# A transformer layer on one core: TensorE's 28 middle units written out without a loop

## The chip, the cores and the metric

The kernel runs on one core of one Trainium2 chip. The metric is the device time of the whole program in microseconds (us). Three timed runs of the kernel before gave 1525.46, 1525.85 and 1527.17 us; the median is 1525.85 us.

A core has five engines that run their own instruction streams and meet only at semaphores: TensorE (PE in the profile, its weight loads PEld), VectorE (DVE), ScalarE (ACT), GpSimd (POOL) and SyncE (SP). A "q" behind the name, as in PEldq or SPq, is the part of an engine that handles register operations, branches, waits and the issue of DMAs.

## The reference

The layer is one attention block and one feed-forward block over hidden states of 4 x 512 x 512 in float32:

```python
x = x + _layernorm(attn(_layernorm(x)))   # 32 query heads, 8 key/value heads, head size 128
x = x + _layernorm(ffn(_layernorm(x)))    # width 1376, silu(gate) * up, then down

# attn: the weights are integer codes with one scale per 128 input rows
w = (codes - 8.0) * repeat(scales, 128)
q, k, v = x @ w_q, x @ w_k, x @ w_v       # rope on q and k, each k/v head serves 4 query heads
p = softmax(q @ k.T * 128 ** -0.5 + causal_mask)
out = (p @ v) @ w_o
```

## The kernel before, in words

Every float32 operand of a matmul is split into a high and a low float16 half, and each product is made of three matmuls (hi x hi, lo x hi, hi x lo), or of two where the weight is exact. The attention runs as 32 units, `UNITS = NKV * NB`: unit U stands for one key/value head and one batch, four units of the same head in a row. A unit has four steps h, one for each query head; head number n is `4 * U + h`. All engines go through the same 32 units, each with a program of its own.

On TensorE (the function `unit` under `@block.tensor`, from line 904) a step issues, in this order:

- `attend` (lines 856 to 869) for head n-2: 30 matmuls of 128 columns, from the transposed probabilities in `ffn_w` into `ps_o`. It waits for `oq_norm` (line 858), `pt_hi_in` and `pt_lo_in` (the two DMA transposes of the probabilities), and `piece_dve`.
- `scores` (lines 841 to 853) for head n+1, into `ps_s`, in three parts, and between these parts
- `out_tile` (lines 934 to 954) for head n-3: the matmuls of the output projection, lines 837 and 838. The first of them waits for `ot_in` at line 942, the DMA transpose of the attention output (`ot<-o_parts` in the rows), and each for its bank of `ps_p`.
- one or two pieces of the next unit's projections (K, V or one of Q0 to Q3; lines 813 to 815 and 829 to 831), and the fourth output tile.

`ps_p` is a ring of four banks that VectorE empties. The two buffers of `wo` and of the projection weights change every four units, so that TensorE's loop body holds NB = 4 units.

The loop is `pe.Fori(0, UNITS // NB - 1)` at line 990: seven passes of four units, with units 0 and 1 ahead of it and units 30 and 31 behind it, these four written out. In the loop the unit number is a value of a register: `NB * p + 2 + i`. So the semaphore count that a wait needs is worked out in a register, and so is the half of the weights, in `half = (V >> 2) & 1` (`project`, `project_v`) and in `output`. The helper `after` (line 153) leaves out a wait that asks for zero when its value is a plain number, and always waits when it is a register's value:

```python
def after(eng, sem, value):
    if isinstance(value, int) and value <= 0:
        return
    eng.wait_ge(sem, value)
```

VectorE has a loop of the same four units a pass (line 1290), ScalarE, GpSimd and SyncE have loops of two units (lines 747, 586 and 457). SyncE issues nearly all DMAs, in the order of its program: in step n the swaps for rope (lines 375, 376), the transposes of the probabilities of head n (lines 385, 391), the transpose of the attention output of head n-2 (line 400), and once a unit the next weights (lines 353, 356, 365). The chain behind one head goes TensorE `scores`, VectorE `lows` (L1152), ScalarE `exps` and `p_high` (L650, L659), GpSimd `p_low` (L511), SyncE's transposes, TensorE `attend`, ScalarE `o_norm` (L667), GpSimd `o_parts` (L519), SyncE's transpose (L400), TensorE `out_tile`.

Of the kernel before, what the change touches and what calls it, by code (L numbers as in the profile page):

```python
# [29 lines left out]
NB, S, D = 4, 512, 512  # L30
# [6 lines left out]
UNITS = NKV * NB  # L37
# [33 lines left out]
FULL = (("K", "Q0"), ("Q1",), ("Q2", "V"), ("Q3",))  # L71
# [92 lines left out]
def layer(nc, x, w_codes, w_scales, o_codes, o_scales,  # L164
          gate_t, gate_s, up_t, up_s, down_t, down_s, cos_t, sin_t, ident_in, mask_in, out):
    ctx = ExitStack()
    with ctx:
# [620 lines left out]
        def _(pe):  # L788
# [198 lines left out]

            unit(0, 0, FULL, first=True)
            unit(1, 1, FULL)
            with pe.Fori(0, UNITS // NB - 1) as p:  # L990
                for i in range(NB):
                    unit(NB * p + 2 + i, (2 + i) % NB, FULL)
            unit(UNITS - 2, NB - 2, FULL)
            unit(UNITS - 1, NB - 1, LAST, last=True)

            outs = outs_before(UNITS) + 3 * KT
# [416 lines left out]
```

## Time and profile before

| | |
|---|---|
| Median of 3 timed runs | 1525.85 us |
| Profiled execution, span from first to last instruction | 1530.4 us |
| TensorE busy | 1427.8 us, 93% of the span, 11104 matmuls |
| VectorE, ScalarE, GpSimd busy | 72%, 65%, 65% |
| Mean granted TensorE clock | 0.983 of full speed |
| Queue q8, kind "instruction" | 109 packets, 1.79 MB |

The profile gives no time of its own for the profiled execution beside the span. The span is 4.55 us longer than the median of the timed runs.

The attention fills the time to about 1290 us, the feed-forward block the rest. TensorE's loop runs from 138 us to 1188 us. The share of busy time says that TensorE is the engine with the least idle time; what the idle time in the loop is made of is told by the waits, the timeline and the windows, whose rows stand below. In such rows a matmul's duration runs to a modelled end: two matmuls of 512 columns in a row start 0.22 us apart although each is shown as 0.38 us long.

### The profile page before, as it was taken

To read this page: it belongs to the slowest core of one execution; us is meant where nothing else is said; L and a number is where in the kernel's file an instruction comes from. 1 tells how busy PE (TensorE), PEld (TensorE's weight loads), DVE (VectorE), ACT (ScalarE), POOL (GpSimd) and SP (SyncE) were. 2 spreads that over 40 slices of the span, in tenths; PEclk is the share of its full clock that TensorE was granted. 3 is DMA by queue.
4 is the path that set the end of the run, shared out by engine and by line. 5 is a ranking of instruction groups with operands and counts; after the bars stand their busy time and mean duration, and the time that the engine had idled before them with its cause. 6 is when DMAs were issued, how large, how long until landed. Compare 5 with 4: busy or idle time off the path is not lost.

```text
span 1530.4 us, 40795 instructions
## 1 busy us (share of the span) xinstructions
PE 1427.8 (93%) x11104; PEld 851.8 (56%) x11104; DVE 1096.3 (72%) x2469; ACT 994.9 (65%) x2582; POOL 1000.8 (65%) x704
## 2 busy tenths in 40 slices
PE   5778899999999999999999999999999967999998
PEld 2444466556556665666566656665666643454543
DVE  7746577777777777777777777777777786776744
ACT  2566577777777777777777777777777862332321
POOL 2467678878887787888788878887888851110100
PEclk9999999999999999999999999999999998999999
DMA  8379989989888888888899888988989864011000
GB/s 268 67 150 163 168 168 173 165 162 169 168 160 165 167 172 160 168 169 167 157 166 169 164 160 162 165 161 158 169 165 172 167 123 91 14 48 42 15 28 28
DMA packets 522609, 217.10 MB, mean 142 GB/s; under 512 B 478944, under 2 KB 480704, under 8 KB 522432
## 3 DMA queue, kind: packets, MB, share of 16 engines
q1 hardware_dynamic: 519968, 210.53, 71.3%
q0 software_dynamic: 2464, 4.23, 1.9%
q8 instruction: 109, 1.79, 0.5%
q14 instruction: 68, 0.56, 0.1%
HBM read 55.32 MB, written 4.19 MB: 39 GB/s over the span
## 4 chain that ended last, share of the span: by engine, by line
PE 71%; DMA 8%; SPq 7%; issue 6%; POOL 3%; DVE 2%; ACT 2%; DVEq 0%; POOLq 0%; ACTq 0%
PE ps_p L813 7%; PE ps_p L815 7%; PE ps_p L814 7%; PE ps_p L837 6%; DMA ot<-o_parts 6%; PE ps_p L838 6%; PE ps_s L1049 4%; PE ps_s L1048 4%; PE ps_s L850 3%; PE ps_s L851 3%; PE ps_s L852 3%; PE ps_o L866 3%; PE ps_o L868 3%; PE ps_o L867 3%; PE ps_p L1062 2%
## 5 line engine op out<-in xcount | busy, mean ns | idle before, releaser
L511 POOL TENSOR_TENSOR p_lo<-prob,p_hi 128x1280 f16<-128x1280 f32 x128 | 335.8, 2623 | 179.2 <-ACT p_hi L659 146.5
L1139 DVE SCALAR_TENSOR_TENSOR y<-ps_p,wo_scale,y 128x512 f32<-128x512 f32 x512 | 380.5, 744 | 81.5 <-PE ps_p L838 79.2
L650 ACT ACTIVATE prob<-prob,exp_bias 128x512 f32<-128x512 f32 (+3 forms) x512 | 285.5, 558 | 12.5
L1152 DVE CUSTOM_DVE_ANT_0 prob<-ps_s,mask 128x512 f32<-128x512 f32 (+3 forms) x512 | 237.0, 482 | 70.5 <-PE ps_s L852 69.4
L813 PE MATMUL ps_p<-x_hi,w_hi 128*128 128x512 f16 x640 | 245.2, 383 | 3.6 <-DVE w_lo L1073 1.5
L837 PE MATMUL ps_p<-ot,wo 128*128 128x512 f16 x512 | 198.8, 388 | 49.9 <-DMA ot<-o_parts 41.7
L814 PE MATMUL ps_p<-x_lo,w_hi 128*128 128x512 f16 x640 | 244.9, 383 | 0.0
L815 PE MATMUL ps_p<-x_hi,w_lo 128*128 128x512 f16 x640 | 244.8, 382 | 0.0
L866 PE MATMUL ps_o<-v_hi,ffn_w 128*128 128x128 f16 x1280 | 221.2, 219 | 9.1 <-DVE rot L1127 8.1
L867 PE MATMUL ps_o<-v_lo,ffn_w 128*128 128x128 f16 x1280 | 221.0, 219 | 0.0
L868 PE MATMUL ps_o<-v_hi,ffn_w 128*128 128x128 f16 x1280 | 221.0, 219 | 0.0
L667 ACT ACTIVATE o_f<-ps_o,inv_sum 128x128 f32<-128x128 f32 x512 | 146.1, 368 | 114.8 <-PE ps_o L868 111.7
L1124 DVE TENSOR_TENSOR other<-ps_p,sin 128x512 f32<-128x512 f32 x160 | 109.5, 685 | 151.7 <-PE ps_p L815 150.4
L495 POOL TENSOR_TENSOR rot<-rot,swap 128x512 f32<-128x512 f32 x160 | 203.3, 1279 | 17.8 <-DMA swap<-other 17.6
L838 PE MATMUL ps_p<-ot,wo 128*128 128x512 f16 x512 | 198.9, 388 | 0.0
L552 POOL TENSOR_TENSOR rstd<-ve,minus_half 128x1 f32<-128x1 f32 x48 | 26.4, 551 | 250.1 <-DVE ve L1209 250.1
L659 ACT ACTIVATE p_hi<-prob 128x1280 f16<-128x1280 f32 x128 | 162.7, 1271 | 23.9 <-DMA ffn_w<-p_hi 19.0
L519 POOL TENSOR_TENSOR o_parts<-o_f,o_parts 128x512 f16<-128x512 f32 x128 | 149.0, 1164 | 38.9 <-ACT o_parts L671 38.9
L503 POOL TENSOR_TENSOR q_lo<-rot,q_hi 128x512 f16<-128x512 f32 x128 | 170.3, 1331 | 2.6 <-ACT q_hi L632 2.6
L850 PE MATMUL ps_s<-k_hi,q_hi 128*128 128x512 f16 (+3 forms) x512 | 155.6, 304 | 9.3 <-POOL q_lo L503 6.8
L851 PE MATMUL ps_s<-k_lo,q_hi 128*128 128x512 f16 (+3 forms) x512 | 155.5, 304 | 0.0
L852 PE MATMUL ps_s<-k_hi,q_lo 128*128 128x512 f16 (+3 forms) x512 | 149.1, 304 | 0.0
(102 smaller groups left out, 2942.5 us busy)
## 6 DMA issues: line engine op xcount, KB each, us to landing
swap<-other SPq DMA_DIRECT2D x320, 128.0 KB, 2.7
w_code<-w_codes SPq DMA_DIRECT2D x36, 384.0 KB, 3.3
w_scale<-w_scales SPq DMA_DIRECT2D x36, 384.0 KB, 4.6
o_code<-o_codes SPq DMA_DIRECT2D x35, 256.0 KB, 2.9
swap<-x SPq DMA_DIRECT2D x16, 256.0 KB, 2.8
out<-z SPq DMA_DIRECT2D x16, 256.0 KB, 2.0
ffn_w<-x SPq DMA_DIRECT2D x3, 1024.0 KB, 9.5
ffn_w<-p_hi SPq DMA_TRANSPOSE x128, 3.5
```

The costliest lines, as they stand in the source:

```text
L511: pool.tensor_tensor(p_lo[:, :], prob[:, hp, :], p_hi[:, :], ALU.subtract).then_inc(p_lod, 1)
L650: act.activation(prob[:, hp, a:a + w], prob[:, hp, a:a + w], ACT.Exp, bias=exp_bias[:, hp, i:i + 1], scale=-1.0, accum_out=exp_sum[:, hp, ...
L813: pe.matmul(ps_p[:, bank, :], wh, xh, start=(k == 0), stop=False)
L814: pe.matmul(ps_p[:, bank, :], wh, xl, start=False, stop=False)
L815: mm = pe.matmul(ps_p[:, bank, :], wl, xh, start=False, stop=(k == KT - 1))
L837: pe.matmul(ps_p[:, bank, :], w, flat(ot[:, hp, 0:TT, :]), start=True, stop=False)
L838: pe.matmul(ps_p[:, bank, :], w, flat(ot[:, hp, TT:2 * TT, :]), start=False, stop=True).then_inc(o_ps, 1)
L866: pe.matmul(o, ph, vh, start=(i == ORDER[0] and j == 0), stop=False)
L867: pe.matmul(o, ph, vl, start=False, stop=False)
L868: mm = pe.matmul(o, pl, vh, start=False, stop=(i == ORDER[-1]))
L1139: dve.scalar_tensor_tensor(tile, ps_p[:, bank, :], scale, tile, ALU.mult, ALU.add).then_inc(o_add, 1)
L1152: dve.tensor_tensor_reduce(prob[:, hp, P_AT[i]:P_AT[i] + w], ps_s[:, bank, col:col + w], mask[:, S - w:], -SCORE_SCALE, NO_MINIMUM, ALU.ad ...
```

## The change

The loop around TensorE's 28 middle units is replaced by a Python `for`, so that these units are written out in the program with plain numbers in place of the register's value. Nothing else is edited; the loops of the other engines stay.

```diff
@@ -987,10 +987,8 @@
 
             unit(0, 0, FULL, first=True)
             unit(1, 1, FULL)
-            with pe.Fori(0, UNITS // NB - 1) as p:
-                for i in range(NB):
-                    unit(NB * p + 2 + i, (2 + i) % NB, FULL)
-            unit(UNITS - 2, NB - 2, FULL)
+            for U in range(2, UNITS - 1):
+                unit(U, U % NB, FULL)
             unit(UNITS - 1, NB - 1, LAST, last=True)
```

The first place is on TensorE, where unit 1 ends and the loop's first unit begins. `L837` and `L838` are the last output tile of unit 1, `L866` to `L868` the first matmuls of `attend`, `ISA` a register operation or wait that the queue handles. Before:

```order
L838 MATMUL ps_p<-ot,wo 128x512
L990 UNCONDITIONAL_BRANCH
L990 ISA
L858 ISA [waits oq_norm]
L860 ISA [waits pt_lo_in,pt_hi_in]
L866 MATMUL ps_o<-v_hi,ffn_w 128x128 [waits piece_dve]
L867 MATMUL ps_o<-v_lo,ffn_w 128x128
```

In the changed kernel:

```order
L837 MATMUL ps_p<-ot,wo 128x512 [waits o_add]
L838 MATMUL ps_p<-ot,wo 128x512
L866 MATMUL ps_o<-v_hi,ffn_w 128x128 [waits pt_lo_in,piece_dve,pt_hi_in,oq_norm]
L867 MATMUL ps_o<-v_lo,ffn_w 128x128
L868 MATMUL ps_o<-v_hi,ffn_w 128x128
```

The branches are gone, and the register operations of `attend` with them; the four waits stand ahead of the first matmul. The matmuls are the same.

The second place is on TensorE in the first unit of the loop body, between the scores and the first output tile, which waits for the transposed attention output. Before:

```order
L843 ISA
L157 ISA [waits rot_lo]
L850 MATMUL ps_s<-k_hi,q_hi 128x512 [waits low_done]
L851 MATMUL ps_s<-k_lo,q_hi 128x512
L852 MATMUL ps_s<-k_hi,q_lo 128x512
L157 ISA
L942 REGISTER_ALU [waits o_add]
L837 REGISTER_ALU [waits ot_in]
L837 REGISTER_ALU
L837 ISA
L837 MATMUL ps_p<-ot,wo 128x512
```

In the changed kernel:

```order
L850 MATMUL ps_s<-k_hi,q_hi 128x512 [waits low_done,rot_lo]
L851 MATMUL ps_s<-k_lo,q_hi 128x512
L852 MATMUL ps_s<-k_hi,q_lo 128x512
L837 MATMUL ps_p<-ot,wo 128x512 [waits ot_in,o_add]
L838 MATMUL ps_p<-ot,wo 128x512
```

The waits for `ot_in` and `o_add` stood on register operations, with two more of these between the wait for `ot_in` and the matmul; now both stand right ahead of the matmul.

## Rows read from the trace of the kernel before

**Rows 1.** The page's busy time by engine, and its slices of the span.

```profile
PE 1427.8 (93%) x11104; PEld 851.8 (56%) x11104; DVE 1096.3 (72%) x2469; ACT 994.9 (65%) x2582; POOL 1000.8 (65%) x704
...
PE   5778899999999999999999999999999967999998
...
PEclk9999999999999999999999999999999998999999
```

**Rows 2.** TensorE's waits, 303 to 1188 us: us in total, times, longest.

```profile
PE ps_p L837 <- DMA ot<-o_parts: 9.9, 16, 1.4
PE ps_o L866 <- DVE rot L1127: 8.1, 5, 1.7
PE ps_p L837 <- issue: 1.5, 4, 0.7
PE ps_o L866 <- DMA ffn_w<-p_lo: 1.0, 1, 1.0
PE ps_p L813 <- issue: 0.4, 2, 0.2
```

**Rows 3.** Queue instructions of line 990: count, duration ns min/median/max, first and last start.

```profile
L990 PEldq COMPARE_BRANCH  x7: 83/4457/4605, 298.7 to 1184.6; - x7
```

**Rows 4.** TensorE's timeline around two loop ends: start us, duration, idle before and releaser.

```profile
301.86 0.38 PE L838 MATMUL ps_p<-ot,wo 128*128 128x512 f16 x1
303.23 0.23 PE L866 MATMUL ps_o<-v_hi,ffn_w 128*128 128x128 f16 x1 [0.99 <-DMA ffn_w<-p_lo]
...
450.75 0.38 PE L837 MATMUL ps_p<-ot,wo 128*128 128x512 f16 x1
450.97 0.38 PE L838 MATMUL ps_p<-ot,wo 128*128 128x512 f16 x1
453.04 0.23 PE L866 MATMUL ps_o<-v_hi,ffn_w 128*128 128x128 f16 x1 [1.70 <-DVE rot L1127]
```

**Rows 5.** The timeline where the loop is left, 1187.4 us on.

```profile
1187.67 0.38 PE L838 MATMUL ps_p<-ot,wo 128*128 128x512 f16 x1
1187.88 0.22 PE L866 MATMUL ps_o<-v_hi,ffn_w 128*128 128x128 f16 x1
```

**Rows 6.** Stretches: length, PE, PEld, DVE, ACT, POOL busy; clock, DMA share, GB/s.

```profile
453.04:599.94 146.90, 143.90 (x1233) 89.79 (x1233) 109.68 (x257) 113.44 (x304) 120.08 (x81) 1.00 0.89 166
599.94:747.29 147.35, 144.06 (x1233) 89.79 (x1233) 109.94 (x257) 113.13 (x304) 120.47 (x81) 1.00 0.89 166
747.29:894.46 147.17, 144.02 (x1233) 89.77 (x1233) 109.61 (x257) 113.33 (x304) 120.22 (x81) 1.00 0.90 166
1042.54:1187.88 145.34, 143.85 (x1232) 89.89 (x1233) 108.03 (x255) 111.81 (x303) 119.84 (x80) 1.00 0.89 166
1187.88:1223.64 35.76, 35.76 (x310) 22.58 (x308) 27.34 (x65) 28.34 (x79) 30.07 (x20) 1.00 0.90 168
```

**Rows 7.** The chain of waits around 541 us and around 1241 us: start, us, what.

```profile
541.23 5.08 DMA ot<-o_parts
546.32 0.24 issue
546.55 0.39 PE ps_p L837
...
1241.72 3.11 DMA ot<-o_parts
1244.83 0.14 issue
1244.97 0.58 PE ps_p L837
```

**Rows 8.** The chain of waits around 484 us.

```profile
483.47 0.22 PE ps_s L852
483.68 0.37 issue
484.06 0.39 PE ps_p L837
```

**Rows 9.** SyncE's timeline around the loop end at 450 us, and the tile that needs it.

```profile
448.77 1.33 SPq L400 DMA_TRANSPOSE ot<-o_parts  x1
...
455.37 0.38 PE L837 MATMUL ps_p<-ot,wo 128*128 128x512 f16 x1
```

**Rows 10.** Instruction fetches of one pass, 453.04 to 599.94 us, and of unit 30.

```profile
q8 instruction: 13, 0.21, 0.6%
...
q8 instruction: 3, 0.05, 0.5%
```

**Rows 11.** The branch of VectorE's loop, with as many passes as TensorE's.

```profile
L1290 DVEq COMPARE_BRANCH  x7: 60/68/68, 302.9 to 1188.7; - x7
```

**Rows 12.** SyncE's waits over the whole span, the three that belong to the loop.

```profile
SPq L390 <- POOL p_lo L511: 82.3, 38, 4.6
SPq L374 <- DVE other L1124: 80.8, 62, 10.1
SPq L399 <- POOL o_parts L519: 73.1, 48, 4.5
```

## The prediction

> **What bounds the kernel now.** I read the page's busy shares first, then TensorE's waits in the loop, then the timeline at the places that the change touches, and last the stretches of one pass each. The page shows TensorE busy 93% of the span with the granted clock near full speed in almost every slice [rows 1]. In the middle of the loop it is denser still: a pass of four units takes 146.90 to 147.35 us, of which 143.90 to 144.06 are busy [rows 6]. VectorE is busy 110 us of such a pass, ScalarE 113, GpSimd 120 and the DMA engines 89%. So TensorE sets the pace, and a pass has only about 3 us in it that are not matmuls.
>
> The waits say what these 3 us are [rows 2]. From 303 to 1188 us, six passes, TensorE idled 9.9 us in 16 waits for the transposed attention output, 8.1 us in five waits ahead of L866 that are put down to VectorE's L1127, 1.0 us in a sixth that is put down to a transpose, and 1.9 us in six waits called issue. The wait ahead of L866 is the one to look at, since L1127 writes `rot`, which `attend` doesn't read. The timeline places it: the last matmul of a pass starts at 450.97, the first of the next pass at 453.04 [rows 4]. The queue has a compare-and-branch of line 990 seven times, with a median of 4457 ns and a minimum of 83 ns [rows 3]. Six of the seven are taken. Where the loop is left, L866 follows L838 after 0.21 us, which is the plain distance of two matmuls, with no idle time at all [rows 5]. So the branch that falls through costs the array nothing, the taken ones hold TensorE's queue for more than 4 us, the array works off about 3 us of matmuls already queued, and the rest is a hole. The releaser named at each hole is only whatever ended last elsewhere.
>
> **The change, part by part.**
>
> Taken branches. One hole is 453.04 - 450.97 = 2.07 us from start to start, less the 0.22 us that the matmul would have taken anyway: 1.85 us. The first is 303.23 - 301.86 - 0.22 = 1.15 us [rows 4]. For the six, the idle times are 8.1 + 1.0 = 9.1 us [rows 2]. Those count from a modelled end that lies 0.38 - 0.22 = 0.16 us after the next possible start, so 6 x 0.16 = 1.0 us comes on top: 10.1 us. A second reading agrees: the last pass, which ends without a taken branch, takes 145.34 us, the three others 147.14 on average, a difference of 1.80 us at equal busy time [rows 6]. I take 10.1 us.
>
> Register operations at a wait. In the loop the first output tile starts 0.24 us after the transpose has landed, outside the loop 0.14 us [rows 7]. The code there is the same but for the register operations, so 0.10 us for each wait that binds: 16 in the waits of six passes [rows 2], 19 by scale for seven, 1.9 us. The waits called issue are the longer form, four register operations: 0.37 us with nothing to wait for [rows 8]. There are four at L837 (1.5 us) and two at L813 (0.4 us) [rows 2]. I count half of these 1.9 us, since a landing a little later may bind there instead. For waits too short for that list I count nothing. That makes 2.8 us, with bounds of 0 (everything is caught by the next landing) and 4.5 us (all of both and 0.7 us for the short ones).
>
> Fetching the program. 28 units in a row are some seven times the code of the loop body. This costs nothing if the loop streams its code already, and it does: one pass fetched 13 packets, 0.21 MB, and the written-out unit 30 fetched 3, the same rate, and was busy 35.76 of 35.76 us while it did [rows 6, 10]. With fewer register operations and no fetch repeated at a branch the total should fall from 109 packets to between 90 and 97. I take 0, with bounds of -1 and +4 us (a stall of 0.05 us at each of some 80 blocks).
>
> What is late next. A transfer that was begun before a loop end and is needed behind it doesn't move when the hole goes. The transposes of the probabilities are needed steps later. The close one is the attention output: issued at 448.77, needed at 455.37 [rows 9], and 1.85 us earlier without the hole, that is at 453.52. One such transpose took 5.08 us to land, another 3.11 [rows 7]; the landing is then at 451.9 to 453.85, so at worst some 0.5 us of the 1.85 turn into a wait. Further back everything is tied to TensorE: SyncE waits mostly for GpSimd's and VectorE's results [rows 12], whose inputs are TensorE's. The hole also lets GpSimd catch up, which is 82% busy in a pass. I put what is given back at 2 us for all six holes together, with bounds of 0 and 10.1 us.
>
> Sum: -10.1 - 2.8 + 0 + 2 = -10.9 us against the profiled span of 1530.4 us, so 1519.5 us. The span lies 4.55 us over the median of the runs, and I assume that offset to stay: 1525.85 - 10.9 = 1514.9 us.
>
> [...]
>
> **The rivals.**
>
> A, the DMA side takes it back. DMA engines are 89% busy in every pass [rows 6], and the waits for `ot` are the largest item in the list [rows 2]. If the pace of SyncE's queue were the true limit, each hole that closes would open as a longer wait for `ot`. For it speaks that 16 such waits exist; against it that unit 30 ran 35.76 us without one idle moment at a share of 0.90 [rows 6], and that those waits last 0.6 us on average (9.9 / 16), as chains that start at TensorE. Full give-back leaves only part of the register term: about 1524 to 1526 us; half of it leaves 1520.
>
> B, slower: the straight code is fetched too late. TensorE needs a new block of code about every 12 us (146.90 / 13 = 11.3) [rows 6, 10]. If the next block came late each time by a time s, some 80 blocks in the former loop would cost 80 s. It decides from 12.9 / 80 = 0.16 us a block; at 0.25 us a block the time is 1525.85 - 12.9 + 20 = 1533 us. For it speaks that the DMA engines that bring the code are 89% busy; against it the dense unit 30, and that the loop's inside shows idle time only at L837, L813 and L866 [rows 2], which are waits in the program and no block borders.
>
> C, a taken branch costs as little as the untaken one and the holes come from a semaphore that is late at each loop end. Then the holes stay, and the register term alone gives 1525.85 - 2.8 = 1523 us. For it speaks the releaser named, L1127; against it that L866 at 1187.88, the same place in the program, has no hole [rows 5]. [...]
>
> D, all waits shrink more than counted, since a reaction sooner on TensorE is a start sooner for the whole chain behind it: all of both terms and nothing given back, -10.1 - 4.5 = -14.6, 1511.3 us.
>
> **How the numbers follow.** The forecast as worked out, from 1512.5 to 1518.5 us, has a chance of 0.70; D and what lies under it 0.10; a half or full give-back (A) 0.12; C 0.04; B 0.04. The range has to hold 8 in 10: from 1511 us (inside D) to 1520.5 us (half of A). A measurement can tell 0.2% from no change, 3.05 us: 1522.8 to 1528.9 us count as the same. Faster are the forecast, D and about half of A's and C's chance: 0.88. The same are the rest of A and C and a weak B: 0.09. Slower: 0.03.
>
> **What would show it.** No compare-and-branch of line 990 in TensorE's queue. No idle time ahead of L866 at the former loop ends, and all passes of four units near 145 us, with TensorE busy 144. The first output tile 0.14 us after its landing in the former loop. The queue q8 with 90 to 97 packets. TensorE's waits for `ot` in the loop still 10 to 12 us: if they are 18 or more, A is right. If idle time appears at places without a wait, in a rhythm of some 12 us, B is. If L866 still has a hole at every sixteenth head, C is. The prediction is wrong if the time is above 1520.5 us, or if it is right by a term that is none of these.

## The result, and the profile after

The changed kernel takes 1516.51 us (median of 5 runs, 1515.25 to 1521.49) against 1525.85 us before: a ratio of 0.9938, 95% interval 0.9918 to 0.9957, or 9.3 us less. In a second group of runs (f0_after) it was 1515.40 us against 1526.38, ratio 0.9927 (0.9911 to 0.9943). The forecast was 1514.9 us, the range 1511 to 1520.5.

The page of the changed kernel answers to [rows 1], its queue q8 to the 109 packets of before:

```profile
PE 1423.1 (94%) x11104; PEld 853.0 (56%) x11104; DVE 1094.0 (72%) x2469; ACT 992.9 (66%) x2582; POOL 1000.6 (66%) x704
...
q8 instruction: 89, 1.46, 0.4%
```

TensorE's waits from the first matmul of unit 6 to that of unit 30, the same six passes as in [rows 2]; columns are us in total, times, longest:

```profile
PE ps_p L837 <- DMA ot<-o_parts: 11.7, 14, 1.6
PE ps_p L813 <- DVE w_lo L1071: 0.4, 2, 0.2
```

The 9.1 us ahead of L866 are gone, and so are the waits called issue. What was 16 waits of 9.9 us for the attention output is now 14 waits of 11.7 us: fewer and longer. Three passes of four units, and the last, answer to [rows 6] (length, then the busy time of PE, PEld, DVE, ACT, POOL, the granted clock, the DMA share):

```profile
443.04:588.25 145.21, 143.50 (x1233) 90.07 (x1232) 109.58 (x257) 112.70 (x305) 120.23 (x80) 1.00 0.87 168
588.25:733.46 145.21, 143.51 (x1234) 90.06 (x1232) 109.55 (x257) 112.95 (x305) 120.22 (x80) 1.00 0.88 168
733.46:881.03 147.57, 144.00 (x1234) 89.86 (x1232) 109.43 (x257) 113.58 (x305) 120.16 (x80) 1.00 0.91 166
...
1026.24:1170.96 144.72, 143.34 (x1233) 90.15 (x1232) 108.99 (x257) 112.93 (x305) 120.23 (x80) 1.00 0.86 167
```

The two profiled spans, 1530.4 and 1513.4 us, differ by 17.0 us, more than the medians. The run of the second profile is 1.85 us longer than its span (1515.25 against 1513.4), and the others are 1.7 to 1.9 us longer, so the profiled execution of before took about 1532.2 us. That is above all five runs of its own group (1525.38 to 1527.73) and about as long as the longest of before in the group of e1_hint (1532.07). To compare what repeats I split the time at the first matmul of units 1, 3 and 31. Of before and of the changed kernel:

```profile
99.60:192.77 93.17, 76.12 (x617) 46.20 (x616) 54.05 (x129) 59.81 (x165) 61.04 (x42) 0.93 0.93 163
192.77:1223.64 1030.87, 1008.14 (x8626) 628.55 (x8624) 767.62 (x1793) 793.34 (x2131) 841.87 (x560) 1.00 0.89 166
```

```profile
99.07:188.27 89.20, 73.62 (x618) 45.13 (x617) 53.68 (x129) 59.71 (x165) 61.02 (x42) 0.94 0.88 170
188.27:1206.72 1018.45, 1005.03 (x8625) 630.18 (x8624) 765.83 (x1793) 791.51 (x2131) 841.48 (x560) 1.00 0.88 167
```

Units 1 and 2, in which the first feed-forward weights are loaded, differ by 4.0 us; in the other profiles below they took from 87.4 to 91.9 us. The 28 units from 3 to 30, called "the stretch" from here on, went from 1030.87 to 1018.45 us, 12.4 us less, and the second profile of the changed kernel has 1018.55. The medians give 9.3 and 11.0 us, so some of the 12.4 may belong to the long execution of before. The six holes alone were 10.1 us in that profile. This looks like the forecast come true. The experiments show that it is not.

### The profile page after: what moved, and what is told of

Its sections match the earlier page's. It is cut to its first block, busy times and chain, and to the rows that moved or that the text cites. A ratio compares the mean times of both kernels' runs of the same rounds, so it can differ in the third digit from the quotient of the medians.

```text
span 1513.4 us, 38106 instructions
## 1 busy us (share of the span) xinstructions
PE 1423.1 (94%) x11104; PEld 853.0 (56%) x11104; DVE 1094.0 (72%) x2469; ACT 992.9 (66%) x2582; POOL 1000.6 (66%) x704
## 4 chain that ended last, share of the span: by engine, by line
PE 69%; DMA 7%; issue 7%; SPq 5%; POOL 5%; DVE 3%; ACT 2%; DVEq 1%; POOLq 0%; ACTq 0%
PE ps_p L813 7%; PE ps_p L815 7%; PE ps_p L814 7%; PE ps_p L837 6%; PE ps_p L838 5%; DMA ot<-o_parts 4%; PE ps_s L1046 4%; PE ps_s L1047 4%; PE ps_s L852 3%; PE ps_s L850 3%; PE ps_s L851 3%; PE ps_o L868 3%; PE ps_o L867 3%; PE ps_o L866 3%; PE ps_p L1060 2%
## 5 line engine op out<-in xcount | busy, mean ns | idle before, releaser
L813 PE MATMUL ps_p<-x_hi,w_hi 128*128 128x512 f16 x640 | 244.6, 382 | 2.8 <-DVE x_lo L1105 1.4
L837 PE MATMUL ps_p<-ot,wo 128*128 128x512 f16 x512 | 198.3, 387 | 48.6 <-DMA ot<-o_parts 42.0
L868 PE MATMUL ps_o<-v_hi,ffn_w 128*128 128x128 f16 x1280 | 221.0, 219 | 0.0
L866 PE MATMUL ps_o<-v_hi,ffn_w 128*128 128x128 f16 x1280 | 221.0, 219 | 0.0
L495 POOL TENSOR_TENSOR rot<-rot,swap 128x512 f32<-128x512 f32 x160 | 202.5, 1274 | 16.8 <-DMA swap<-other 16.8
L838 PE MATMUL ps_p<-ot,wo 128*128 128x512 f16 x512 | 198.6, 388 | 0.0
L850 PE MATMUL ps_s<-k_hi,q_hi 128*128 128x512 f16 (+3 forms) x512 | 155.3, 303 | 8.0 <-POOL q_lo L503 5.5
```

The source lines that it names most:

```text
L813: pe.matmul(ps_p[:, bank, :], wh, xh, start=(k == 0), stop=False)
L837: pe.matmul(ps_p[:, bank, :], w, flat(ot[:, hp, 0:TT, :]), start=True, stop=False)
L838: pe.matmul(ps_p[:, bank, :], w, flat(ot[:, hp, TT:2 * TT, :]), start=False, stop=True).then_inc(o_ps, 1)
L866: pe.matmul(o, ph, vh, start=(i == ORDER[0] and j == 0), stop=False)
L868: mm = pe.matmul(o, pl, vh, start=False, stop=(i == ORDER[-1]))
```

## The experiments

The stretch by kernel (one profile each), the matmul-to-matmul time lost in it at holes ahead of L866 and at all other waits over 0.2 us, and the ratio of the timed runs to those of before. Loss is the distance of two starts less the distance that such a pair has without a wait. A profile is of one execution, up to 5.2 us over the median of its runs (f4_bothhint, 1523.45 against 1518.26), so a stretch by itself tells no differences of a few us.

| kernel | stretch us | holes | other waits | ratio, 95% interval |
|---|---|---|---|---|
| before | 1030.87 | 10.06 | 18.87 | |
| the change | 1018.45 | 0 | 16.83 | 0.9938 (0.9918 to 0.9957) |
| the change, second group (f0_after) | 1018.55 | 0 | 17.06 | 0.9927 (0.9911 to 0.9943) |
| TensorE's loop with a hint (e1_hint) | 1028.66 | 0 | 26.52 | 0.9988 (0.9976 to 1.0000) |
| single passes, registers kept (e2_single) | 1024.27 | 0 | 22.74 | 0.9968 (0.9955 to 0.9982) |
| four passes, rest written out (e3_half) | 1023.34 | 4.90 | 16.53 | 0.9952 (0.9935 to 0.9968) |
| loop end behind attend (e4_edge) | 1060.48 | 28.5, ahead of L850 | | 1.0199 (1.0181 to 1.0218) |
| the change, near branches (e5_short) | 1023.14 | 0 | 21.10 | 0.9939 (0.9917 to 0.9962) |
| TensorE, VectorE written out (f1_both) | 1009.97 | 0 | 8.55 | 0.9855 (0.9833 to 0.9878) |
| the change, VectorE's loop with a hint (f3_dvehint) | 1009.30 | 0 | 7.90 | 0.9865 (0.9843 to 0.9887) |
| both loops with a hint (f4_bothhint) | 1022.11 | 0 | 20.05 | 0.9944 (0.9926 to 0.9962) |
| only VectorE written out (f2_dve) | 1029.68 | 6.55 | 21.07 | 0.9989 (0.9975 to 1.0004) |
| all five written out (f5_all) | 1009.98 | 0 | 8.4 | 0.9837 (0.9812 to 0.9861) |
| both written out, padded (f6_pad) | 1018.91 | 0 | 15.09 | 0.9926 (0.9905 to 0.9948) |

**e1_hint: the branch without the wait for its code.**

```diff
-            with pe.Fori(0, UNITS // NB - 1) as p:
+            with nc.Fori(0, UNITS // NB - 1, engines=[pe.engine], hint_back_edge=True) as p:
```

> The loop of before is kept, with a prefetch hint for the branch at its end. Measure: the stretch from the first matmul of unit 3 to that of unit 31, 1030.9 us in the profile of before and 1018.5 us in that of the changed kernel, and the median time. Theory (a taken branch waits for the code of the loop's top to be fetched, and the hole is that time less the matmuls already queued): the six branches fall from 4.4 us to under 1 us, the holes ahead of L866 to under 0.3 us, the register operations stay; stretch 1020 to 1022 us, time 1517 to 1520 us. Rival (a taken branch on TensorE is slow by itself, or a semaphore is late at the loop end): the holes stay at 1.2 to 1.9 us, stretch 1030 us, time 1525 to 1527 us.

The median was 1526.11 us, 1.8 us under the 1527.93 us of before in its group. The queue's instructions of line 990 (count, duration ns min/median/max) answer to [rows 3]:

```profile
L990 PEldq BRANCH_PREFETCH_HINT  x7: 36/36/45, 134.3 to 1030.6; - x7
L990 PEldq COMPARE_BRANCH  x7: 88/353/389, 294.6 to 1177.7; - x7
```

TensorE's waits from unit 3 to 31 (us in total, times, longest):

```profile
PE ps_p L837 <- DMA ot<-o_parts: 16.7, 23, 1.7
PE ps_p L837 <- issue: 2.3, 6, 0.7
```

The mechanism holds: a hinted branch takes 0.35 us instead of 4.46, and no hole is left ahead of L866. So I take the 4.46 us for a wait for code; in e5_short below a taken branch to a loop head a few instructions back lasted 0.21 to 0.24 us. But the time hardly fell, and did not reach the theory's 1517 to 1520 us; it is the rival's time, without the rival's holes: the other waits grew from 18.9 to 26.5 us. 10.1 us of holes were taken away and 7.7 came back.

**e2_single: no branch back, all register operations.**

```diff
-            with pe.Fori(0, UNITS // NB - 1) as p:
-                for i in range(NB):
-                    unit(NB * p + 2 + i, (2 + i) % NB, FULL)
+            for q in range(UNITS // NB - 1):
+                with pe.Fori(q, q + 2, 2) as p:
+                    for i in range(NB):
+                        unit(NB * p + 2 + i, (2 + i) % NB, FULL)
```

> Seven loops of a single pass in a row: every group of four units is written out, but the unit number is still a register's value, so all register operations stay and no branch back is taken. Theory (register operations cost 0.1 to 0.3 us at each wait that binds, 2 to 3 us in all): no hole ahead of L866, the first output tile still 0.24 us after its landing, stretch from unit 3 to unit 31 1020.5 to 1021.5 us, 2 to 3 us over the changed kernel; time 1517 to 1520 us. Rival (only the branches count, what the register operations delay is caught by the next landing): stretch 1018 to 1019 us, time as the changed kernel, 1516.5 us.

Median 1522.04 us, 4.9 us under before by the ratio. The stretch is 5.8 us longer than that of the changed kernel, not 2 to 3 (4.6 us by the ratios): registers cost about twice what I had counted. Set against e1_hint, which has the same register operations and a hinted branch, it is 4.4 us shorter (3 us by the ratios, whose intervals overlap). It had 99 fetches where e1_hint had 104; why the two differ stays open.

**e3_half: three taken branches instead of six.**

```diff
-            with pe.Fori(0, UNITS // NB - 1) as p:
+            with pe.Fori(0, 4) as p:
                 for i in range(NB):
                     unit(NB * p + 2 + i, (2 + i) % NB, FULL)
-            unit(UNITS - 2, NB - 2, FULL)
+            for U in range(18, UNITS - 1):
+                unit(U, U % NB, FULL)
```

> The loop does four passes (three taken branches), units 18 to 30 are written out. Theory: about half of the gain, three holes of 1.2 to 1.9 us (4.6 us in all) and the register operations of 16 units: stretch from unit 3 to unit 31 1024 to 1025 us, time 1520 to 1522 us. Rival (the DMA side takes back what is gained, so that the gain is no sum over holes): units 18 to 31 show waits for the attention output that are longer by as much as the holes that are gone, and the stretch from unit 18 on is no shorter than in before (476.3 us).

Median 1521.00 us, stretch 1023.34 us. From unit 18 to unit 31 it took 471.1 us (740.94 to 1212.05) against 476.3 before, so part of the gain is kept where the loop is gone. It keeps three fifths of the gain by the stretches (7.5 of 12.4 us) and three quarters by the ratios (7.3 of 9.5 us), both more than the theory's half; the intervals of the ratios reach 2.5 to 3 us to either side.

**e4_edge: the same loop, its end behind short matmuls.**

```diff
+            attend_ahead(2, 2)
             with pe.Fori(0, UNITS // NB - 1) as p:
                 for i in range(NB):
-                    unit(NB * p + 2 + i, (2 + i) % NB, FULL)
-            unit(UNITS - 2, NB - 2, FULL)
+                    unit(NB * p + 2 + i, (2 + i) % NB, FULL, attended=(i == 0))
+                attend_ahead(NB * p + 6, 2)
+            unit(UNITS - 2, NB - 2, FULL, attended=True)
```

`attend_ahead` issues the first `attend` of the unit, which `unit` then leaves out.

> The loop is kept but its end moved behind the 30 short matmuls (56 ns each) of the first attend of a unit. Theory (hole = branch time less the matmuls queued at it): some 14 matmuls are queued, now worth 0.8 us in place of 3 us, so each of six holes grows from 1.7 to about 3.7 us and stands behind the last L868 instead of ahead of the first L866; stretch from unit 3 to 31 about 1041 us, time 1536 to 1538 us, less what the waits for the attention output catch. Rival (a semaphore that attend waits for is late at each fourth unit): the hole stays ahead of L866 at 1.2 to 1.9 us, time 1525 to 1527 us.

Median 1557.69 us, 30 us over before, more than forecast. The branch at its new line:

```profile
L996 PEldq COMPARE_BRANCH  x7: 83/5111/5949, 298.0 to 1213.5; - x7
```

TensorE's waits, 300 to 1165 us:

```profile
PE ps_s L850 <- issue: 14.7, 3, 5.2
PE ps_s L850 <- POOL q_lo L503: 12.8, 3, 4.3
```

And the 12 us around one loop end, in the columns of the passes above:

```profile
600.50:612.50 12.00, 7.27 (x48) 3.96 (x47) 6.47 (x10) 5.44 (x16) 6.81 (x4) 0.76 1.06 183
```

The holes moved with the branch to where it now stands, and grew from 1.7 to 4.7 us on average: 27.5 us by these rows, which count from modelled ends, and 0.16 us more for each. The matmuls queued ahead of the branch are short, and the branch itself took 4.9 to 5.9 us instead of 4.0 to 4.6. So the hole goes with the branch and the work queued ahead of it, and no semaphore of the first `attend` makes it; three of the six are put down to `q_lo`, but all six have the branch in front. The rest of the loss is the clock: the granted clock was 0.76 in the 12 us around this hole and 0.72 to 0.86 in the same stretch of the five others. It was 0.50 for 3.4 us at three of the six holes and for 6.8 us at the other three (at this one from 606.7 to 613.5 us), and matmuls of 512 columns in a row started 0.43 us apart there instead of 0.22; in the kernel before it was 1.00 in each pass [rows 6]. So TensorE's busy time in the stretch rose from 1008.14 to 1019.12 us.

**The second theory.** The waits that came back in e1_hint are not spread evenly. In the changed kernel 11.1 of the 16.8 us lie in units 6, 10, 14, 18, 22 and 26, the units that begin a pass of the loops still kept. In e1_hint it is 11.7 of 26.5 and in e2_single 12.0 of 22.7; in the kernel before these six units had 5.2 us of such waits beside the 10.1 us of holes. So in these three kernels, where TensorE's holes are gone and VectorE's loop is as it was, 6 to 7 us come back in the very units behind the holes. The chain of waits of the changed kernel leads from there to VectorE (start, us, what):

```profile
443.89 0.07 DVEq L1288
443.95 0.28 issue
444.24 0.74 DVE y L1137
444.98 2.50 DVE w_lo L1071
447.47 0.39 issue
447.86 0.07 DVEq L1288
447.94 0.05 issue
...
449.62 0.55 DVE prob L1150
450.17 1.56 issue
451.73 0.06 DVE low L1150
...
453.91 0.67 DVE other L1122
...
459.11 1.68 SPq L391
...
461.07 3.74 DMA ot<-o_parts
464.81 0.14 issue
464.95 0.38 PE ps_p L837
```

L1288 is the head of VectorE's loop. Its branch at 443.89 is shown as 0.07 us, yet the first instruction behind it, of the same line, starts at 447.86, 3.97 us later. I read this as a wait for code like TensorE's, only that VectorE's record of the branch, 0.07 us, doesn't contain the wait. Two instructions already queued cover most of it, then VectorE stands still, and once more for 1.56 us at 450.17. The DMA packets show the fetches: on queue q14, whose packets of 8 KB become fewer when VectorE is written out (68 on the page, 42 in f1_both), one started 2.15 us after this branch and the next 6.0 us after it. In the kernel before the first of them started 2.3 to 2.6 us behind each of VectorE's six taken branches. The row that shows VectorE's stall in the kernel before, 300 to 1170 us, is

```profile
DVE low L1152 <- issue: 8.7, 6, 2.1
```

In the changed kernel the stall delays the scores' minimum, then the rope of the next pieces, then SyncE's queue, and ends at 464.95 as a wait of TensorE of 1.59 us. In the kernel before, both engines fetched at the same loop end, and by this theory TensorE's hole hid VectorE's.

**f1_both, f3_dvehint and f4_bothhint, with f0_after as their measure.** f0_after is the changed kernel again. f1_both adds

```diff
-            with dve.Fori(0, UNITS // NB - 1) as p:
-                for i in range(NB):
-                    unit(NB * p + 2 + i, (2 + i) % NB, FULL)
-            unit(UNITS - 2, NB - 2, FULL)
+            for U in range(2, UNITS - 1):
+                unit(U, U % NB, FULL)
```

f3_dvehint instead keeps VectorE's loop as `nc.Fori(..., engines=[dve.engine], hint_back_edge=True)`, and f4_bothhint is the kernel before with such a hint on both loops.

> The changed kernel again, as the measure for the other runs of this group. Time 8 to 11 us under before; stretch from the first matmul of unit 3 to that of unit 31 within 2 us of 1018.5 us.

> TensorE's and VectorE's middle units are both written out. New theory: VectorE's loop end is a fetch too (its branch is shown as 68 ns, but its queue starts the next operation 4.5 us later, and VectorE then idles 1 to 2 us in a wait called issue); TensorE's hole covered it, and in the changed kernel it comes back as a wait for the attention output of 1.8 to 2.2 us in units 6, 10, 14, 18, 22, 26. By it these waits fall under 1 us: stretch from unit 3 to 31 1007 to 1012 us, time 6 to 11 us under the changed kernel. Rival (the DMA side sets these waits): they stay, stretch 1016 to 1019 us, time within 2 us of the changed kernel.

> The changed kernel, VectorE's loop kept with a prefetch hint for its branch: only the fetch is taken away, VectorE's register operations stay. New theory: VectorE's queue goes on within 1 us of the branch, the waits of 1.8 to 2.2 us in units 6, 10, ..., 26 fall under 1.2 us, time 4 to 8 us under the changed kernel. Rival (DMA side, or VectorE's register operations rather than its fetch): time within 2 us of the changed kernel.

> Both loops kept, both with a prefetch hint; all register operations stay. With the hint on TensorE alone the time fell only 1.8 us. New theory: with VectorE's fetch gone too the six holes really go, time 7 to 11 us under before. Rival (the register operations on TensorE were the larger part of the change): time 1 to 3 us under before, as with the hint on TensorE alone.

Medians 1515.40, 1505.59, 1505.18 and 1518.26 us, against 1526.38 us before. TensorE's waits from unit 3 to 31 with the hint on VectorE (f3_dvehint):

```profile
PE ps_p L837 <- DMA ot<-o_parts: 4.8, 7, 1.1
PE ps_p L837 <- issue: 0.8, 1, 0.8
```

VectorE's waits called issue in it, 300 to 1165 us:

```profile
DVE prob L1150 <- issue: 0.3, 1, 0.3
```

And in the changed kernel, 300 to 1170 us:

```profile
DVE low L1150 <- issue: 7.9, 6, 2.2
...
DVE prob L1150 <- issue: 4.7, 5, 1.2
```

So 12.6 us of standing still on VectorE became 0.3, and TensorE's other waits fell from 17.1 to 7.9 us; in the six units behind the loop ends they fell from 11.4 us (f0_after) to 1.4, to 0.9 with VectorE written out and to 0.3 with both hints. VectorE's queue did not go on within 1 us of the branch, as expected, but after 2.0 to 3.4 us, its first code packet started 0.1 to 1.6 us behind the branch, and the gain of 10 us was above the 4 to 8 expected. The hint does as much as writing VectorE out (0.9865 and 0.9855, their intervals overlap), so it is the fetch and not VectorE's register operations. This edit is worth some 10 us on top of the change, as much as the change that this study is about. With both hints and all registers (f4_bothhint) the time is 8.1 us under before, where the hint on TensorE alone had brought 1.8: the holes are worth their price once the stall beneath them is gone too.

**f2_dve: the cover from the other side.** The kernel before with VectorE's edit of f1_both alone.

> The kernel before with VectorE's middle units written out and TensorE's loop kept. Theory (the two engines' fetches lie at the same loop end and cover each other): TensorE's six holes of 1.2 to 1.9 us stay and hide most of what VectorE's were worth, time 0 to 4 us under before, where the same edit was worth 9.8 us on top of the changed kernel. Rival (the two are independent sums): 8 to 11 us under before.

Median 1528.48 us against 1529.38, ratio 0.9989 (0.9975 to 1.0004). The same edit that is worth 10 us beside the change is worth nothing measurable without it. TensorE's holes shrank from 10.1 to 6.6 us, and its other waits rose by 2.2. Of two stalls that lie over each other, taking away either alone gains at most 1 to 2 us (the interval of this one holds zero, that of e1_hint touches it), and both together 8.1 us (f4_bothhint).

**f5_all: the other three engines.** ScalarE's, GpSimd's and SyncE's loops written out as well.

> All five engines' middle units written out. The branches of ScalarE, GpSimd and SyncE delay the next queue operation by only 0.26 to 0.33 us, fourteen times each, and their register operations 0.04 to 0.1 us each. Theory (these lie in the chain from the scores to the transpose that TensorE waits for): 1 to 4 us under the kernel with TensorE and VectorE written out. Rival (they have idle time beside the chain): within 1 us of it.

Median 1505.49 us, ratio 0.9837 (0.9812 to 0.9861); f1_both in its own group had 0.9855 (0.9833 to 0.9878). The intervals overlap, and the stretches are equal (1009.98 and 1009.97 us). No gain is shown. The ratios by themselves would leave room for one of 2 to 3 us; the equal stretches speak for the rival.

**f6_pad: a longer program without register operations.** To f1_both it adds, in `project` four times and in `project_v` six times for each k,

```diff
+                    if V > 2:
+                        for _ in range(4):
+                            pe.sem_inc(pe_passed)
```

> TensorE's and VectorE's middle units written out as in the earlier run, and TensorE's program made longer again by some 104 semaphore increments a unit that nobody waits for, placed among the projection matmuls where they hide, none at a wait. Theory (the register operations also cost by the length of the program: a 16 KB fetch of TensorE's code that meets the transpose of the attention output lands it 0.8 to 1.0 us later, and a longer program has more of them): 109 fetches where the changed kernel has 89, waits for the attention output up, time 2 to 6 us over the kernel with both written out. Rival (the register operations cost only what stands between a landing and the matmul): time within 1.5 us of it.

Median 1518.42 us, ratio 0.9926, so 11 us over f1_both by the ratios. It doesn't settle its question. It had 101 fetches, not 109, and the waits for the attention output became fewer, not more. The rows are TensorE's waits in it, 300 to 1160 us:

```profile
PE ps_p L814 <- DVE w_lo L1078: 0.9, 3, 0.4
PE ps_p L844 <- issue: 0.9, 5, 0.2
```

Instead every unit loses 0.28 us on average ahead of the same output tile, and 0.18 us more in the V piece, whose matmuls start 56 ns apart: the increments did not hide where I had put them. What it shows is that some 0.46 us a unit lost in TensorE's queue, 13 us in 28 units, made the stretch 9 us longer (1018.91 against 1009.97).

**e5_short: a branch to code that is there.** The changed kernel with this behind units 5, 9, 13, 17, 21 and 25:

```diff
+                if U % NB == 1 and U < UNITS - 3:
+                    with pe.Fori(0, 2) as p:
+                        pass
```

> The changed kernel with a loop of two passes and an empty body on TensorE at each of the six former loop ends, so that a branch is taken there to code that is already loaded. Theory (only the fetch costs): the branches take 0.05 to 0.4 us, no hole ahead of L866, time within 2 us of the changed kernel. Rival (any taken branch empties TensorE's queue for 4 us): six holes of 1 to 2 us, time 5 to 10 us over the changed kernel.

Ratio 0.9939 (0.9917 to 0.9962), as the change itself.

```profile
L993 PEldq COMPARE_BRANCH  x12: 76/142/237, 295.2 to 1030.5; - x12
```

Each loop's first branch is taken and lasted 207 to 237 ns, the second falls through in 76 ns, and no hole stood ahead of L866. Queue q8 has 89 packets, as in the changed kernel, so these branches added no fetch. Its stretch in the one profile was 4.7 us longer than the changed kernel's. That profile is of the longest of its six runs (1524.22 us, median 1520.75); 4.3 us of the difference lie in waits, and after one of 1.96 us, which ended at 479 us, the granted clock fell: it was 0.86 from 478 to 490 us. The ratios show no difference.

## Why the prediction was right, and where it was not

The time lay in the range, and the sum of -10.9 us against a measured -9.3 us is close. Two of its four terms were wrong, in opposite directions, so that the closeness is in part luck.

Taken branches, -10.1 us. Right in size and cause. The holes measured 10.06 us and went. e1_hint shows that they were the wait for code (the branch fell from 4.46 to 0.35 us and no hole was left), e4_edge that queued work is what covers them (with matmuls of 56 ns queued at the branch the holes grew from 1.7 to 4.7 us), and e5_short that a taken branch takes 0.21 to 0.24 us where it adds no fetch, and an untaken one 76 ns. On VectorE the same is seen by the next instruction, 4.2 to 4.5 us behind the branch in the kernel before and 2.0 to 3.4 us with a hint.

What is late next, +2 us. Wrong in size, and wrong in what it left out. I looked at the transfer in flight at a loop end and found at most 0.5 us; that transfer was indeed no trouble. What I passed over was VectorE, whose branch I took to be over in the 68 ns of its record [rows 11]. On that engine the record doesn't contain the wait for code. The next instruction of the loop started 4.2 to 4.5 us after the branch in the kernel before too, and VectorE's own wait called issue, 8.7 us in six times, would have led there. With the hint alone 7.7 of 10.1 us came back, 6.5 of them in the six units behind the loop ends; in f4_bothhint, with VectorE's stall gone as well, these units kept 0.3 us of waits.

Register operations, -2.8 us. Too small. The reaction to a landing went from 0.24 to 0.14 us as said [rows 7], as in the row at 464.81 above. But e2_single, which keeps the register operations and takes no branch back, has a stretch 5.8 us longer than the change (4.6 us by the ratios). Register operations and a hinted loop together cost 10.2 us (e1_hint against the change; 7.6 by the ratios) and 12.8 (f4_bothhint against f3_dvehint; 12.1). The hinted branch takes 0.35 us of TensorE's queue six times, and no hole stood behind it. It is not the reaction alone. One thing beside it is the number of waits: 28 over 0.2 us in f4_bothhint, 10 in f3_dvehint. Counted in their traces, of the waits for the attention output that began its first tile late, 21 of 22 and 9 of 9 had a 16 KB fetch of TensorE's code overlap the transfer waited for, but only 33 of 90 and 27 of 103 of the tiles that did not wait. A transfer that met a fetch landed in 4.4 and 4.2 us (medians) instead of 3.1. In the changed kernel, where VectorE's stall makes waits of its own, it was 8 of 15 late tiles and 24 of 97 others. With registers and the loop the program is fetched in 104 packets instead of 89. f6_pad was to test this and did not. So the coincidence is measured and the cause stays open.

Fetching the program, 0 us. Right that straight code costs nothing against the loop; there was no rhythm of stalls without a wait. The number of fetches was 89, just under the 90 to 97 given.

The rivals. B (late code) did not happen: in the loop the changed kernel shows waits only at L837 and L813, and no rhythm of stalls. C (no fetch behind the branch) is refuted by e1_hint and e4_edge. A (the DMA side takes the gain back) described what e1_hint shows, but its reason was wrong: with VectorE's stall gone the same waits fall by 9 us at a DMA share of 0.89, so the DMA engines' load did not set them.

How much is the branches' and how much the registers' depends on the order. By e1_hint the branches were worth -2.2 us of stretch and the rest of the change -10.2; by e2_single it is -6.6 and -5.8. I had -8.1 (10.1 less the 2 given back) and -2.8. A count by place needs no order: in the six units behind the loop ends, holes and waits together fell from 15.3 to 11.1 us, 4.2 us less, and in the 22 others the waits fell from 13.7 to 5.7 us, 8.0 us less. By every count the branches gave less than I had and the register operations more. The two errors nearly cancel; that the time came out right is no proof of the working.

The offset of 4.55 us between span and median was no constant. A run is 1.85 us longer than its span, and the profiled execution of before was simply a long one. It didn't matter for the sum, which is a difference.

## What to carry to other kernels

Look for a wait for code at each pass of a loop with a long body, on each engine that has one. Here it was 4.0 to 4.6 us on TensorE and 4.2 to 4.5 us on VectorE, whose passes have some 2913 and 653 records in the trace of the kernel before, and did not appear on ScalarE, GpSimd and SyncE, with 286, 159 and 171, whose queues went on after 0.26 to 0.33 us; whether the length of the pass decides it was not tested. Read it from the start of the next instruction behind the branch, not from the branch's own duration, and try a prefetch hint as well as writing the loop out: on VectorE it did as much. Stalls of several engines at one point of the program can cover each other (here the medians fell 0.9 and 1.8 us with either stall gone alone, f2_dve and e1_hint, and 8.1 us with both, f4_bothhint), so price an edit by what the other engines do in the same microseconds, and expect the second edit to bring what the first did not. Here the change together with a hint on VectorE's loop (1505.18 us) or with VectorE written out too (1505.59 us) beats both kernels, 21 us under before.

## What the runs showed of the hardware

- TensorE's taken branch back took 3.98 to 4.61 us in the kernel before (3.6 to 4.4 in f2_dve, 4.9 to 5.9 in e4_edge), with a hint 0.34 to 0.39 us, and to a loop head a few instructions back 0.21 to 0.24 us; an untaken one 76 to 88 ns in e5_short, the kernel before and e1_hint. VectorE's queue went on 4.2 to 4.5 us after its branch in the kernel before, 3.1 to 5.3 us in the two profiles of the changed kernel, and with a hint after 2.0 to 3.4 us, which its queued work covered. ScalarE's, GpSimd's and SyncE's queues, with loops of two units, went on after 0.26 to 0.33 us.
- A transpose of the attention output landed in 3.1 us (median of the stretch, in each of the 14 profiles) when no 16 KB fetch of TensorE's code overlapped it, and in 3.9 to 4.4 us when one did (32 to 56 of 112 transfers). That the fetch is the reason is not shown.
- The granted clock was 0.50 for 3.4 to 6.8 us in or right behind each of the six holes of 4.4 to 5.3 us on TensorE in e4_edge (0.72 to 0.86 on average over 12 us), and two matmuls of 512 columns in a row started 0.43 us apart there instead of 0.22; the holes of 1.2 to 1.9 us in the kernel before left it at 1.00. Behind a wait of 1.96 us in e5_short it was 0.50 for 3.4 us (0.86 over 12 us).
